# x's groups 8 to 11 ahead of Wv's second half, and a new order of the staged pieces

## The chip, the cores and the metric

One Trainium2 chip, 8 cores, one launch. Every core computes one of the 8 batch entries with the full weights, and no core talks to another. The metric is the device time in microseconds (us) of the slowest core. One core has TensorE (PE), VectorE (DVE), ScalarE (ACT), GpSimd (POOL) and SyncE (SP), and 16 DMA engines, which serve a queue of hardware-made transfers (issued here by SP) and one of software-made transfers (issued by GpSimd; these can cast f32 to bf16 on the way).

## What is computed

x is [8, 2048, 1024] f32. An adaptive-layernorm block: the vector c gives six modulation vectors, x goes through a linear attention with relu features, then through a quantized linear layer. Cut to what matters:

```python
mod = (silu(c) @ wmod).reshape(8, 6, 1, 1024)
sa, ca, ga, sb, cb, gb = (mod[:, k] for k in range(6))
ga, gb = (sign(g) * maximum(abs(g), 0.25) for g in (ga, gb))
h = layernorm(x) * (1 + ca) + sa
q = relu(h @ Wq.T) / 8;  k = relu(h @ Wk.T) / 8      # 16 heads of 64
v = h @ Wv.T;            u = silu(h @ Wu.T)
kv = k.T @ v             # per head, over all 2048 tokens
x = x + ga * ((srms_norm(q @ kv) * u) @ Wo.T)
h = layernorm(x) * (1 + cb) + sb
x = x + gb * (int8_linear(h, weight) + bias)
```

## The kernel before

A core's 2048 tokens are 16 groups of 128 (g), and four chunks of 512 (i). The first half of the kernel makes kv, which needs all tokens. For each chunk: `stats(g)` (VectorE, then three small GpSimd operations) and `xhat(g)` (ScalarE) normalize a group of x, `transp` turns it on TensorE into h1, `kproj` and `vproj` are eight products each (a unit is eight 128x512 matmuls into one PSUM bank, evicted by ScalarE), and `kvprod` adds to kv. The order of issue is written out by hand, and every engine works through its own instructions strictly in that order. In a loop over `eight`, unit n is (half, j): the first four units use the first half of the weight, the last four the second. The second half of the kernel makes Q, U, the heads, Wo, the second layernorm and the quantized layer chunk by chunk (`xunit`, `wproj`, `norm1`, `fproj`). Its first stage needs VectorE early: `qproj(0, ec)` is evicted by VectorE from ec = 2 on (L665), and the head product `ohead(0, 2)` (L692) needs that.

Three streams of loads lie around the change.

GpSimd issues, in this order: Wk's second half (four pieces), Wv's first half, x's groups 8 and 9, Wv's second half, groups 10, 11, 12 (L566 to L573); then, behind the statistics of groups 8 to 11, groups 13 to 15 as their buffers come free (`more_x`). A weight half is 2 MiB of f32 in HBM and is cast to bf16.

SP issues the staged pieces: 24 loads of 1 MiB in three buffers, in the order of the list `stream`: ga, sb, cb (four each), Wo (four), gb (four), the FFN weight (four). `AT` holds where each begins. The first three wait for Wv's first half (L575); each later one waits until the piece three before it is consumed (`staged`).

VectorE consumes them. `mod_piece(v, c)` multiplies a piece of wmod by silu(c) and sums it into a column (two operations, L436); after the fourth piece `mod_fin` finishes the vector. `wo_piece(c)` multiplies two rows of Wo's piece by ga (L479) and needs ga as a row, `row_g`. `ffn_quant` takes the last four. `mod()` takes the next entry of the list `mods` (16 wmod pieces with the four of Wo behind the twelfth). Before, it is called in all eight units of V of chunk 0, in all eight of V of chunk 1, and in the first four of K of chunk 2.

A finished column becomes a row of all partitions by `row(v, dst)`: a small DMA to HBM (`put`) and a broadcast back (`get`), both issued by GpSimd, with the wait for the put's landing between them. Before, `row(0)` stands in V of chunk 1, and between V of chunk 1 and K of chunk 2 stand Wq's first half, `row(1)`, Wq's second half, `row(2)` and both halves of Wu, all on GpSimd. `row(3)` goes into row_g again and therefore waits for the last Wo piece (`fold_tok`). `fill()` writes row_gbb to the whole output, four loads of SP behind the last FFN piece.

Of the kernel before, what the change touches and what calls it, by code (L numbers as in the profile page):

```python
# [13 lines left out]
D = 1024  # L14
# [3 lines left out]
NC = 8  # L18
# [54 lines left out]
def build_nc():  # L73
# [3 lines left out]
    def dram(name, shape, dt=F32, kind="ExternalInput"):  # L77
        return nc.dram_tensor(name, shape, dt, kind=kind)
# [8 lines left out]
    d_wb = dram("wmod_b", [128, 4, NC, D])  # L87
# [10 lines left out]
    def sb(name, shape, dt=F32, at=None):  # L98
        nbytes = int(np.prod(shape[1:])) * size[dt]
        off = cur[0] if at is None else at  # L100
        if at is None:
            cur[0] = off + ((nbytes + 31) // 32) * 32
        assert off + nbytes <= CAP, f"SBUF overflow: {name} {off + nbytes - CAP}"
        return nc.alloc_sbuf_tensor_at(name, list(shape), dt, offset=off)
# [7 lines left out]
    wv = sb("wv_s", [128, 2, NC, 512], BF16)  # L112
    wq_at = cur[0]
    wq = sb("wq_s", [128, 2, NC, 512], BF16)
    wu = sb("wu_s", [128, 2, NC, 512], BF16)
    wo = sb("wo_s", [128, NC, D], BF16)
# [3 lines left out]
    row_g = sb("row_g", [128, D])  # L120
    row_cb = sb("row_cb", [128, D])
    row_sb = sb("row_sb", [128, D])
    row_gbb = sb("row_gbb", [128, D])
# [18 lines left out]
    mod_c = [sb(f"mod_c{v}", [128, NC]) for v in range(4)]  # L142
# [5 lines left out]
    gbb_c = sb("gbb_c", [128, NC])  # L148
# [66 lines left out]
    def x_prev(g):  # L215

        return g - 2 * XR if g - XR in xe else g - XR

    def load_x(q, key, g, after):
        s = key % XR  # L220
        if key in xe:
            x_tok[key] = q.dma(sl_e[key], xe[key][:], bass.AP(d_x, g * 128 * D, [[D, 128], [1, D]]), *after)
            return
        x_tok[key] = q.dma(sl_x[q][s], xr[s][:],
                           bass.AP(d_x, g * 128 * D, [[D, 128], [1, D]]), *after)

    w_tok = {}
# [7 lines left out]
    def load_w(w, dst, hf, *after):  # L235
        w_tok[w, hf] = POOL.dma(sl_w[w, hf], dst[:, hf],
                                bass.AP(d_w[w], hf * NC * 512,
                                        [[2 * NC * 512, 128], [512, NC], [1, 512]]), *after)
# [1 line left out]
    st_tok = {}  # L240
    st_free = {}
    wa_free = {}
    stream = ([(d_wb, (v * NC + 2 * c) * D, 4 * NC * D) for v in range(3) for c in range(4)]
              + [(d_wo, 2 * c * D, NC * D) for c in range(4)]
              + [(d_wb, (3 * NC + 2 * c) * D, 4 * NC * D) for c in range(4)]
              + [(d_fw, 2 * c * D, NC * D) for c in range(4)])
    AT = {"ga": 0, "sb": 4, "cb": 8, "wo": 12, "gb": 16, "ffn": 20}

    def load_stage(n, *after):

        if n < len(stream):
            src, off, row = stream[n]
            st_tok[n] = SP.dma(sl_s[n % SR], stage[n % SR][:], bass.AP(src, off, [[row, 128], [1, 2048]]),
                               st_free.get(n - SR), wa_free[NC - 1], *after)

    def staged(n, t):

        st_free[n] = t
        load_stage(n + SR)
# [52 lines left out]
    def xhat(g):  # L312

        i, j = divmod(g, 4)
        x = xbuf(g)
        xh_tok[g] = x_free[g] = ACT.do(lambda e: e.activation(  # L316
            out=xh[j][:], in_=x[:], func=AF.Identity, scale=rt[j][:, 0:1], bias=nmr[j][:, 0:1]),
            nm_tok[g], tp_tok.get((i - 1, 3)), t_silr if g < 2 else None)
# [42 lines left out]
    def take():  # L361
        b = ring["banks"][ring["n"] % len(ring["banks"])]
        ring["n"] += 1
        return b, ring["free"].get(b)

    def mm8(lhs, rhs, bank, *after, each=None):
        for dc in range(NC):
            t = PE.do(lambda e, dc=dc: e.matmul(pb[bank][:], lhs(dc), rhs(dc),  # L368
                                                start=(dc == 0), stop=(dc == NC - 1)),
                      *after, each(dc) if each else None, inc=(dc == NC - 1))  # L370
        return t
# [5 lines left out]
    def kbuf(i, j):  # L377
        return kT1[j] if i == 1 else kT[j]
# [29 lines left out]
    def vproj(i, hf, j):  # L408
        b, free = take()
        t = vp_tok[i] = mm8(lambda dc: h1[:, i, dc, 128 * j:128 * j + 128], lambda dc: wv[:, hf, dc],  # L410
                            b, free, w_tok["wv", hf])
        v_tok[i, j] = ring["free"][b] = ACT.do(lambda e: e.copy(  # L412
            out=vT[j][:, 512 * hf:512 * hf + 512], in_=pb[b][:]), t, kv_tok.get((i - 1, j)))

    def kvprod(i, j):
        for p in range(NC):
            t = PE.do(lambda e, p=p: e.matmul(
                pb[p // 4][:, 128 * (p % 4):128 * (p % 4) + 128],
                kbuf(i, j)[:, 128 * p:128 * p + 128], vT[j][:, 128 * p:128 * p + 128],
                start=(i == 0 and j == 0 and p % 4 == 0),  # L420
                stop=(i == NT - 1 and j == 3 and p % 4 == 3)),
                k_tok[i, j], v_tok[i, j], k_free[0], k_free[1], inc=(p == NC - 1))
        kv_tok[i, j] = t
# [3 lines left out]
    row_tok, col_tok = {}, {}  # L427
    fold_tok = [None]
    put_tok = {}

    def mod_piece(v, c):

        n = AT[("ga", "sb", "cb", "gb")[v]] + c
        s = stage[n % SR]
# [7 lines left out]
    def put(k, col, *after):  # L442

        put_tok[k] = POOL.dma(sl_p[k], bass.AP(d_rows, k * D, [[NC, 128], [1, NC]]), col[:], *after)

    def get(k, row, *after):

        row_tok[k] = POOL.dma(sl_g[k], row[:], bass.AP(d_rows, k * D, [[0, 128], [1, D]]),
                              put_tok[k], *after)
# [20 lines left out]
    def row(v, dst, *after):  # L470
        put(v, mod_c[v], col_tok[v])
        get(v, dst, *after)

    def wo_piece(c):

        n = AT["wo"] + c
        s = stage[n % SR]
        for d in range(2):
            t = DVE.do(lambda e, d=d: e.tensor_tensor(  # L479
                out=wo[:, 2 * c + d], in0=s[:, 1024 * d:1024 * d + 1024], in1=row_g[:], op=ALU.mult),  # L480
                st_tok[n], row_tok[0])
        fold_tok[0] = t
        staged(n, t)
# [3 lines left out]
    def ffn_quant(ec):  # L487

        c, d = divmod(ec, 2)
        n = AT["ffn"] + c  # L490
        w = stage[n % SR][:, 1024 * d:1024 * d + 1024]
# [70 lines left out]
    def more_x(g):  # L562
        load_x(POOL, g, g, (x_free[x_prev(g)],))
# [2 lines left out]
    for c in range(4):  # L566
        load_wk(1, c, wa_tok[6, 1])
    load_w("wv", wv, 0)
    for g in (8, 9):
        more_x(g)  # L570
    load_w("wv", wv, 1)
    for g in (10, 11, 12):
        more_x(g)  # L573
    for n in range(SR):
        load_stage(n, w_tok["wv", 0])  # L575

    def piece(v, c):
        mod_piece(v, c)
        if c == 3:
            mod_fin(v)  # L580

    mods = [lambda v=v, c=c: piece(v, c) for v in range(4) for c in range(4)]
    mods[12:12] = [lambda c=c: wo_piece(c) for c in range(4)]

    def mod():
        if mods:
            mods.pop(0)()
# [5 lines left out]
    for n, (hf, j) in enumerate(eight):  # L593
        vproj(0, hf, j)
        if 1 < n < 6:
            xhat(6 + n)
            if n < 5:
                more_x(11 + n)
        mod()
        if n >= 5:  # L600
            kvprod(0, n - 5)
    for n, (hf, j) in enumerate(eight):
        vproj(1, hf, j)
        if n == 0:
            kvprod(0, 3)
        if n >= 5:
            kvprod(1, n - 5)
        if n < 4:
            transp(2, n)
            stats(12 + n)  # L610
        if n == 3:
            row(0, row_g)
        mod()

    load_w("wq", wq, 0, wa_free[NC - 1])
    row(1, row_sb)
    load_w("wq", wq, 1)
    row(2, row_cb)
    for h in range(2):
        load_w("wu", wu, h)  # L620
    for n, (hf, j) in enumerate(eight):
        kproj(2, hf, j)
        if n == 0:
            kvprod(1, 3)
        if n < 4:
            mod()
        else:
            xhat(8 + n)
    row(3, row_g, fold_tok[0])
    put(4, gbb_c, col_tok[3])  # L630
    get(4, row_gbb)
    for n, (hf, j) in enumerate(eight):
        vproj(2, hf, j)
        if n >= 5:
            kvprod(2, n - 5)
        if 1 < n < 6:
            transp(3, n - 2)
# [396 lines left out]
```

How the kernel before makes its waits and increments, by code:

```python
    def emit(self, eng):  # L47
        seen = {}
        for after, fn, sem, step in self.items:
            need = {}
            for s, v in after:
                if v > need.get(s.name, (s, 0))[1]:
                    need[s.name] = (s, v)
            for s, v in need.values():
                if v > seen.get(s.name, 0):
                    eng.wait_ge(s, v)
                    seen[s.name] = v
            if fn is None:
                continue
            ins = fn(eng)
            if sem is not None:
                ins.then_inc(sem, step)
```

## Time and profile before

| | |
|---|---|
| time, median of 3 runs | 458.42 us (458.16 to 458.9) |
| the profiled execution | 458.85 us; its slowest core's span 457.3 us |
| spans of the 8 cores | 450.7 to 457.3 us |
| TensorE busy | 390.0 us, 85% of the span |
| VectorE, ScalarE, GpSimd busy | 60%, 52%, 21% |
| HBM read, written | 70.36 MB, 24.67 MB |
| chain that ended last | PE 45%, DMA 17%, VectorE 13%, ScalarE 7% |

The profile is that of one execution; times in it are microseconds from the core's first instruction, and are those of the slowest core (core 4) where no other is named. The DMA share is the mean busy share of the core's 16 DMA engines. A number in brackets behind an instruction is the idle time of its engine just before it, and what ended that.

### The profile page before, as it was taken

What the parts mean: (1) busy time and instruction counts of PE and PEld (TensorE: products, weight loads), DVE (VectorE), ACT (ScalarE), POOL (GpSimd) and SP (SyncE); (2) the same over time, 40 slices, a digit from 0 to 9 for tenths busy, and PEclk for the clock granted to TensorE, in tenths of its full rate; (3) what the DMA queues carried; (4) which work ended last, traced back from release to release, by engine and by line L of the source; (5) the groups of instructions that cost most, each with busy time, mean ns of one, the idle gap of its engine ahead of it and who ended that gap; (6) DMA issues with size and microseconds to landing.
All of it is one profiled execution on the core that took longest, in us unless ns stands there. A gap on an engine that the chain in (4) does not pass through costs nothing.

```text
span 457.3 us, 6430 instructions; the slowest of 8 cores (450.7 to 457.3 us)
## 1 busy us (share of the span) xinstructions
PE 390.0 (85%) x2022; PEld 185.4 (41%) x2062; DVE 273.9 (60%) x487; ACT 235.6 (52%) x342; POOL 96.9 (21%) x148
## 2 busy tenths in 40 slices
PE   3043799849998999988898899999999999999983
PEld 1020444425544545434443344444444443444432
DVE  4557902175692644467845875568565755766885
ACT  3342553527257433768656854476825577443532
POOL 2514701040064011000011202121212131202421
PEclk9995699979999999998999999999999999999999
DMA  7999699949985999999698615634564574265796
GB/s 194 280 262 335 159 171 245 330 131 299 339 303 185 195 311 292 216 245 352 200 365 273 130 46 96 137 84 101 93 120 93 110 139 85 64 128 94 125 149 140
DMA packets 20914, 87.05 MB, mean 190 GB/s; under 512 B 2825, under 2 KB 3089, under 8 KB 17042
## 3 DMA queue, kind: packets, MB, share of 16 engines
q0 software_dynamic: 8544, 31.49, 37.9%
q1 hardware_dynamic: 12338, 55.16, 36.0%
q8 instruction: 17, 0.28, 0.3%
q14 instruction: 15, 0.12, 0.1%
HBM read 70.36 MB, written 24.67 MB: 208 GB/s over the span
## 4 chain that ended last, share of the span: by engine, by line
PE 45%; DMA 17%; DVE 13%; issue 8%; ACT 7%; SPq 6%; POOL 3%; DVEq 0%; ACTq 0%; POOLq 0%
PE pb L368 32%; PE pb L842 8%; DMA xr<-x_tm 8%; SPq L44 6%; DMA wa<-wmod_a 5%; DMA stage<-wmod_b 5%; DVE stage L436 3%; ACT rn L704 2%; DVE h L790 2%; DVE am L793 2%; DVE wm_c L492 2%; PE pb L702 1%; DVE bn L302 1%; ACT rn L707 1%; PE pb L819 1%
## 5 line engine op out<-in xcount | busy, mean ns | idle before, releaser
L368 PE MATMUL pb<-h,wu_s 128*128 128x512 bf16 x251 | 61.5, 386 | 1.6 <-ACT u_s L681 1.2
L368 PE MATMUL pb<-wo_s,u_s 128*128 128x512 bf16 x251 | 59.4, 379 | 1.2 <-DVE u_s L684 1.0
L842 PE MATMUL pb<-fq,xqT 128*128 128x512 bf16 (+1 forms) x255 | 58.7, 372 | 1.7 <-ACT xqT L824 1.3
L368 PE MATMUL pb<-wv_s,h 128*128 128x512 bf16 x249 | 59.2, 387 | 0.9 <-ACT kT L384 0.4
L368 PE MATMUL pb<-h,wq_s 128*128 128x512 bf16 x249 | 59.6, 379 | 0.4
L436 DVE SCALAR_TENSOR_TENSOR stage<-stage,silr 128x1024 f32<-128x1024 f32 x32 | 37.7, 1219 | 20.8 <-DMA stage<-wmod_b 20.8
L368 PE MATMUL pb<-wk_s,h 128*128 128x512 bf16 x203 | 45.4, 379 | 0.6 <-DMA wk_s<-wk 0.3
L709 DVE SCALAR_TENSOR_TENSOR q_s<-rn,pb 128x512 bf16<-128x512 f32 x32 | 22.0, 686 | 29.7 <-ACT rn L707 29.3
L302 DVE BATCH_NORM_STATS2 bn<-xr 128x6 f32<-128x512 f32 x26 | 16.7, 684 | 37.0 <-DMA xr<-x_tm 37.0
L368 PEld LDWEIGHTS pb<-h,wu_s 128*128 128x128 bf16 x256 | 24.9, 99 | 31.1 <-issue 4.5
L368 PEld LDWEIGHTS pb<-wo_s,u_s 128*128 128x128 bf16 x256 | 24.9, 98 | 31.0 <-issue 1.4
L368 PEld LDWEIGHTS pb<-h,wq_s 128*128 128x128 bf16 x256 | 24.8, 98 | 28.9 <-issue 0.2
L842 PEld LDWEIGHTS pb<-fq,xqT 128*128 128x128 bf16 x264 | 25.1, 98 | 27.6 <-issue 1.7
L368 PEld LDWEIGHTS pb<-wv_s,h 128*128 128x128 bf16 x256 | 24.7, 99 | 28.2 <-issue 2.7
L681 ACT ACTIVATE u_s<-pb 128x512 bf16<-128x512 f32 x32 | 18.6, 593 | 26.3 <-PE pb L368 26.2
L669 ACT ACTIVATE q_s<-pb 128x512 bf16<-128x512 f32 x26 | 15.5, 596 | 31.4 <-PE pb L368 23.6
L316 ACT ACTIVATE xh<-xr,nmr,rt 128x1024 bf16<-128x1024 f32 x13 | 16.1, 1240 | 29.9 <-POOL nmr L308 29.9
L412 ACT CAST vT<-pb 128x512 bf16<-128x512 f32 x32 | 18.4, 585 | 25.1 <-PE pb L368 25.0
L368 PEld LDWEIGHTS pb<-wk_s,h 128*128 128x128 bf16 x208 | 20.1, 98 | 24.1 <-issue 0.8
L44 POOL DMA_DIRECT2D out_tm<-h x15 | 13.5, 897 | 76.7 <-DVE h L846 63.0
L384 ACT ACTIVATE kT<-pb 128x512 bf16<-128x512 f32 x26 | 15.5, 596 | 27.3 <-PE pb L368 27.3
L305 POOL TENSOR_SCALAR rt<-mv 128x1 f32<-128x1 f32 x16 | 9.9, 618 | 88.6 <-DVE mv L304 87.0
(104 smaller groups left out, 577.2 us busy)
## 6 DMA issues: line engine op xcount, KB each, us to landing
stage<-wmod_b SPq DMA_DIRECT2D x16, 1024.0 KB, 11.6
xr<-x_tm SPq DMA_DIRECT2D x21, 512.0 KB, 4.6
wa<-wmod_a SPq DMA_DIRECT2D x16, 512.0 KB, 20.7
out_tm<-row_gbb SPq DMA_DIRECT2D x4, 2048.0 KB, 17.4
out_tm<-xr POOLq DMA_DIRECT2D x15, 512.0 KB, 7.9
out_tm<-h POOLq DMA_DIRECT2D x15, 512.0 KB, 5.3
xr<-x_tm POOLq DMA_DIRECT2D x8, 512.0 KB, 19.8
stage<-wo SPq DMA_DIRECT2D x4, 1024.0 KB, 6.2
```

The lines of the kernel that those rows point to most:

```text
L44: lambda e: e.dma_start(out=out, in_=in_, **how), slot.sem, 16))
L302: t = DVE.do(lambda e, hf=hf: e.bn_stats(out=bn6[j][:, 6 * hf:6 * hf + 6], in_=x[:, 512 * hf:512 * hf + 512]), x_tok[g])
L305: t = POOL.do(lambda e: e.tensor_scalar(out=rt[j][:], in0=mv[j][:, 1:2], scalar1=1e-5, scalar2=None, op0=ALU.add), t, xh_tok.get(g - 4))
L316: xh_tok[g] = x_free[g] = ACT.do(lambda e: e.activation(out=xh[j][:], in_=x[:], func=AF.Identity, scale=rt[j][:, 0:1], bias=nmr[j][:, 0:1] ...
L368: t = PE.do(lambda e, dc=dc: e.matmul(pb[bank][:], lhs(dc), rhs(dc), start=(dc == 0), stop=(dc == NC - 1)), *after, each(dc) if each else ...
L384: k_tok[i, j] = ring["free"][b] = ACT.do(lambda e: e.activation(out=kbuf(i, j)[:, 512 * hf:512 * hf + 512], in_=pb[b][:], func=AF.Relu, sc ...
L412: v_tok[i, j] = ring["free"][b] = ACT.do(lambda e: e.copy(out=vT[j][:, 512 * hf:512 * hf + 512], in_=pb[b][:]), t, kv_tok.get((i - 1, j)))
L436: col_tok[v] = DVE.do(lambda e, d=d: e.scalar_tensor_tensor(out=s[:, D * d:D * d + D], in0=s[:, D * d:D * d + D], scalar=1.0, in1=silr[:], ...
L669: q_tok[i, ec] = ring["free"][b] = ACT.do(lambda e: e.activation(out=q_s[:, ec], in_=pb[b][:], func=AF.Relu, scale=0.125), t, vp_tok[NT - ...
L681: u_tok[i, ec] = ring["free"][b] = ACT.do(lambda e: e.activation(out=u_s[i % 2][:, ec], in_=pb[b][:], func=AF.Silu), t, vp_tok[NT - 1], kv ...
L709: ot_tok[n] = o_free[b] = DVE.do(lambda e: e.scalar_tensor_tensor(out=q_s[:, p], in0=rn[n % 2][:], scalar=1e12, in1=pb[b][:], op0=ALU.min, ...
L842: t = PE.do(lambda e, ic=ic, sl=sl, ps=ps: e.matmul(ps, xqT[a][:, ic], fq[:, ic, sl], start=(ic == 0), stop=(ic == NC - 1)), free, xqT_tok ...
```

## The change

x's groups 10 and 11 are issued before Wv's second half, and the staged pieces wait for Wv's second half instead of its first. In the stream, gb's pieces stand ahead of Wo's. `mod()` is called in the last three units of V of chunk 0, the last four of V of chunk 1 (behind the statistics of groups 12 to 15), in all eight units of K of chunk 2 and in V of chunk 2 until the list is empty. The rows and the loads of Wq and Wu are issued within these loops: row 0 and Wq's first half in the fifth unit of V of chunk 1, row 1 and Wq's second half in the first unit of K of chunk 2, row 2 and both halves of Wu in its fifth, the puts of gb and of gb x bias with the get of row_gbb in the first unit of V of chunk 2, and the get of gb's row in its fifth. Nothing is added to the computation and nothing taken from it.

```diff
--- before.py
+++ after.py
@@ -240,11 +240,10 @@
     st_tok = {}
     st_free = {}
     wa_free = {}
-    stream = ([(d_wb, (v * NC + 2 * c) * D, 4 * NC * D) for v in range(3) for c in range(4)]
+    stream = ([(d_wb, (v * NC + 2 * c) * D, 4 * NC * D) for v in range(4) for c in range(4)]
               + [(d_wo, 2 * c * D, NC * D) for c in range(4)]
-              + [(d_wb, (3 * NC + 2 * c) * D, 4 * NC * D) for c in range(4)]
               + [(d_fw, 2 * c * D, NC * D) for c in range(4)])
-    AT = {"ga": 0, "sb": 4, "cb": 8, "wo": 12, "gb": 16, "ffn": 20}
+    AT = {"ga": 0, "sb": 4, "cb": 8, "gb": 12, "wo": 16, "ffn": 20}
 
     def load_stage(n, *after):
 
@@ -566,13 +565,12 @@
     for c in range(4):
         load_wk(1, c, wa_tok[6, 1])
     load_w("wv", wv, 0)
-    for g in (8, 9):
+    for g in range(8, 12):
         more_x(g)
     load_w("wv", wv, 1)
-    for g in (10, 11, 12):
-        more_x(g)
+    more_x(12)
     for n in range(SR):
-        load_stage(n, w_tok["wv", 0])
+        load_stage(n, w_tok["wv", 1])
 
     def piece(v, c):
         mod_piece(v, c)
@@ -580,7 +578,7 @@
             mod_fin(v)
 
     mods = [lambda v=v, c=c: piece(v, c) for v in range(4) for c in range(4)]
-    mods[12:12] = [lambda c=c: wo_piece(c) for c in range(4)]
+    mods += [lambda c=c: wo_piece(c) for c in range(4)]
 
     def mod():
         if mods:
@@ -596,8 +594,8 @@
             xhat(6 + n)
             if n < 5:
                 more_x(11 + n)
-        mod()
         if n >= 5:
+            mod()
             kvprod(0, n - 5)
     for n, (hf, j) in enumerate(eight):
         vproj(1, hf, j)
@@ -608,29 +606,35 @@
         if n < 4:
             transp(2, n)
             stats(12 + n)
-        if n == 3:
+        else:
+            mod()
+
+        if n == 4:
             row(0, row_g)
-        mod()
-
-    load_w("wq", wq, 0, wa_free[NC - 1])
-    row(1, row_sb)
-    load_w("wq", wq, 1)
-    row(2, row_cb)
-    for h in range(2):
-        load_w("wu", wu, h)
+            load_w("wq", wq, 0, wa_free[NC - 1])
     for n, (hf, j) in enumerate(eight):
         kproj(2, hf, j)
         if n == 0:
             kvprod(1, 3)
-        if n < 4:
-            mod()
-        else:
+        if n > 3:
             xhat(8 + n)
-    row(3, row_g, fold_tok[0])
-    put(4, gbb_c, col_tok[3])
-    get(4, row_gbb)
+        mod()
+        if n == 0:
+            row(1, row_sb)
+            load_w("wq", wq, 1)
+        if n == 4:
+            row(2, row_cb)
+            for h in range(2):
+                load_w("wu", wu, h)
     for n, (hf, j) in enumerate(eight):
         vproj(2, hf, j)
+        mod()
+        if n == 0:
+            put(3, mod_c[3], col_tok[3])
+            put(4, gbb_c, col_tok[3])
+            get(4, row_gbb)
+        if n == 4:
+            get(3, row_g, fold_tok[0])
         if n >= 5:
             kvprod(2, n - 5)
         if 1 < n < 6:
```

## Rows read from the trace of the kernel before

**Rows 1.** Spans of the cores, and mean granted TensorE clock.

```profile
core 2: 455.2 us, clock 0.966
...
core 4: 457.3 us, clock 0.966
```

**Rows 2.** Timeline, TensorE, core 4: start, us, operation, [idle before <-releaser].

```profile
77.53 10.52 PE L368 MATMUL pb<-wv_s,h 128*128 128x512 bf16 x47
...
92.22 0.61 PE L417 MATMUL pb<-vT,kT 128*128 128x128 bf16 x8 [1.99 <-ACT vT L412]
...
100.16 1.01 PE L417 MATMUL pb<-vT,kT 128*128 128x128 bf16 x8 [5.61 <-ACT vT L412]
...
100.97 3.62 PE L368 MATMUL pb<-wv_s,h 128*128 128x512 bf16 x8
...
141.90 0.44 PE L326 MATMUL pb<-id_b,xh 128*128 128x128 bf16 x5 [1.31 <-ACT xh L316]
```

**Rows 3.** Timeline, ScalarE, core 4.

```profile
98.30 1.24 ACT L316 ACTIVATE xh<-xr,nmr,rt 128x1024 bf16<-128x1024 f32 x1 [6.23 <-POOL nmr L308]
```

**Rows 4.** Timeline, VectorE, core 4, group 11's statistics.

```profile
91.94 1.29 DVE L302 BATCH_NORM_STATS2 bn<-xr 128x6 f32<-128x512 f32 x2 [3.27 <-DMA xr<-x_tm]
```

**Rows 5.** Timeline, GpSimd, core 4: loads issued, one small result.

```profile
53.73 0.56 POOL L44 DMA_DIRECT2D wv_s<-wv  x1
...
55.29 0.60 POOL L44 DMA_DIRECT2D wv_s<-wv  x1
...
55.81 1.65 POOL L44 DMA_DIRECT2D xr<-x_tm  x3
...
96.47 1.74 POOL L308 TENSOR_SCALAR nmr<-mv,rt 128x1 f32<-128x1 f32 x1 [0.18 <-POOL rt L307]
...
98.15 1.69 POOL L44 DMA_DIRECT2D xr<-x_tm  x3
```

**Rows 6.** Landings of the two loads of Wv (tile wv_s), core 4.

```profile
DMA to landing us min/median/max: 16.8/21.6/26.4
```

**Rows 7.** Windows: three of core 4, two of core 2; clock, DMA share, GB/s last.

```profile
60.00:90.00 30.00, 29.53 (x141) 13.48 (x142) 4.49 (x9) 12.77 (x21) 2.92 (x8) 1.00 1.01 254
...
90.00:105.00 15.00, 7.40 (x41) 3.79 (x40) 10.45 (x18) 4.24 (x6) 5.96 (x7) 0.77 0.52 165
...
122.00:155.00 33.00, 30.98 (x189) 15.89 (x191) 19.37 (x36) 19.16 (x28) 12.81 (x16) 1.00 0.82 244
...
90.00:105.00 15.00, 8.38 (x50) 4.55 (x49) 11.41 (x23) 3.41 (x5) 5.68 (x6) 0.77 0.64 185
...
122.00:155.00 33.00, 31.88 (x193) 16.45 (x196) 19.40 (x34) 19.15 (x28) 12.79 (x16) 1.00 0.82 221
```

**Rows 8.** Timeline, VectorE: last staged piece, first Q eviction; core 4, then 2.

```profile
183.56 1.22 DVE L436 SCALAR_TENSOR_TENSOR stage<-stage,silr 128x1024 f32<-128x1024 f32 x1
...
189.75 0.69 DVE L665 TENSOR_SCALAR q_s<-pb 128x512 bf16<-128x512 f32 x1 [3.58 <-PE pb L368]
...
182.28 1.22 DVE L436 SCALAR_TENSOR_TENSOR stage<-stage,silr 128x1024 f32<-128x1024 f32 x1
...
187.22 0.69 DVE L665 TENSOR_SCALAR q_s<-pb 128x512 bf16<-128x512 f32 x1 [2.33 <-PE pb L368]
```

**Rows 9.** DMA queues in 122:140, 147:156 and 189:208: packets, MB, share.

```profile
q1 hardware_dynamic: 797, 5.79, 89.8%
...
q0 software_dynamic: 237, 1.29, 87.1%
...
q0 software_dynamic: 285, 1.81, 54.0%
...
q1 hardware_dynamic: 549, 3.01, 46.6%
```

**Rows 10.** Timeline, GpSimd, core 4: the get of row_cb.

```profile
180.44 0.54 POOL L44 DMA_DIRECT2D row_cb<-rows  x1 [18.71 <-DMA rows<-mod_c]
```

**Rows 11.** Timeline, TensorE, core 4: third head product.

```profile
192.30 0.38 PE L692 MATMUL pb<-q_s,kv_bd 128*128 128x512 bf16 x1
```

## The prediction

> **What bounds the kernel now.** I began with the spans of the cores [rows 1]: core 4 is the slowest, core 2 stands 2.1 us below it. The profiled execution took 458.85 us, 1.55 more than core 4's span and 0.43 more than the median of the runs (458.42). The sums below are in core 4's span and are shifted at the end.
>
> Then TensorE in order of time [rows 2]. It is nearly full except around the first V product. There it stands still twice for an eviction of V, 1.99 and 5.61 us, and its granted clock is at the lower of its two levels afterwards, 1.2 GHz instead of 2.4: eight 512-column products take 3.62 us at 100.97, where 47 take 10.52 before (1.79 for eight), and eight small ones 1.01 instead of 0.61. A third wait, 1.31 us at 141.90, is for a normalized group.
>
> Who made the evictions late is seen one engine at a time. ScalarE [rows 3] stood 6.23 us in front of the normalization of group 11, and the V evictions queue behind it. That waited for GpSimd's small result, which ended at 98.2; it waited for VectorE's statistics, which waited for x's group 11 to land at 91.94 [rows 4]. Group 11 was issued at 55.8 with four others behind both halves of Wv [rows 5], and shared the last stretch with three staged pieces, released when Wv's first half landed (53.73 + 16.8 = 70.5) [rows 5, 6]. GpSimd could not issue groups 13 to 15 before 98.15, since they stand behind the late statistics.
>
> Last the windows [rows 7] and VectorE's order [rows 8]. The transfer engines are 0.52 busy in 90 to 105 and 0.82 in 122 to 155, and full in 60 to 90. In the second, VectorE waits for the row of ga with all three staged buffers full. So 15 x 0.48 + 33 x 0.18 = 7.2 + 5.9 = 13.1 us of transfer time are unused on core 4, 5.4 + 5.9 = 11.3 on core 2. The staged pieces end at 183.56 + 1.22 = 184.8 on VectorE, and the next thing in its order, the eviction of the third Q product, waits only 3.58 us for TensorE [rows 8]. This is the margin that matters: the staged pieces are a second path, just behind TensorE's.
>
> **The change part by part.** *Groups 10 and 11 ahead of Wv's second half.* Groups 8 and 9 follow Wv's first half (70.5) at once, groups 10 and 11 now follow them: four groups of half a MiB. A staged MiB costs 0.898 x 18 us = 16.2 us for 5.79 MB, 2.9 us [rows 9]; with the other stretches I take 3.1. So group 11 lands near 70.5 + 6.2 = 77, 15 us earlier, and ScalarE comes to it after six units, near 77.53 + 6 x 1.79 = 88. Both stalls (7.6 us) and the slow clock behind them (1.8 + 0.4 = 2.2) go. The price is that Wv's second half comes 3.1 us of transfer later. It landed at 55.3 + 26.4 = 81.7 + issue, about 82.2 [rows 5, 6], with three pieces taking part of the engines. Without them I put it at 81 to 82; it is wanted after four units, 77.53 + 4 x 1.79 = 84.7 [rows 2]. Margin 3 us; bounds are nothing and the 3.1 us minus that margin, so nothing.
>
> *Pieces only after Wv's second half.* The first leaves at 81 to 82 instead of 70.5. In a full queue this delays nothing by itself: what moves out of the way of one moves into the way of the other.
>
> *Pieces consumed from V's sixth unit, none before group 2's four statistics are done.* The pieces before those statistics are 3 instead of 12. In transfers, three pieces and groups 12 to 15 are 5 MiB, 82 + 5 x 3.1 = 97.5, so the statistics run near 98 to 105, ahead of ScalarE, which comes to them in the second half of K of chunk 2, near 117. The 1.31 us wait goes. VectorE's own work is the same; it is on no path here.
>
> *gb's pieces ahead of Wo's, row_g and the weights issued from within the loops.* ga is complete after the first piece behind the statistics, near 108, and row_g is back some 8 us later (an estimate, less than half of the 18.71 below, as no weight is ahead of it), long before Wo's pieces are due. The 5.9 us hole goes. On GpSimd each row is a put, a wait for its landing, a get and then the next weight load. The wait before row_cb was 18.71 us, with half a weight ahead of the put in the queue [rows 10]. By that, now: row_g and Wq's first half leave near 116; sb is complete near 117, its put lands behind Wq near 133; cb's near 152; then both halves of Wu leave, near 153 where it was 181. They are wanted near 192. puts 3 and 4 and their gets queue behind Wu, and nothing on GpSimd waits for them until the second layernorm. The output fill can start earlier, behind the last FFN piece in SP's order; it writes 8 MiB under products that wait for no load, so I cost it at nothing; if that cover is gone, the FFN piece is late, a MiB at 3.1 us.
>
> **The sum.** TensorE's path gains 7.6 + 2.2 + 1.3 = 11.1 us. Without more, the third Q product's eviction would be possible at 189.75 - 11.1 = 178.7, and the head product that needs it would come at 192.30 - 11.1 = 181.2 [rows 8, 11].
>
> VectorE's pieces end, by differences: 184.8 - 13.1 (holes) + 2 (new holes: the start behind Wv, the catch-up after the statistics) + what now goes ahead of the last Wo piece and did not before (both halves of Wu and row_cb) - 4 (FFN's first piece and the start of its second, which went ahead and no longer do). For Wu the row of 189 to 208 gives 0.54 x 19 = 10.3 us for 1.81 MB written, 5.9 us a half; that of 147 to 156 gives 0.871 x 9 = 7.8 us, less 1.6 for row_g, for 0.77 MB, 8.5 us a half [rows 9]. I take 6.5, nearer to the first, where both queues were at work as they will be; both halves 13, with row_cb 14.6. End: 184.3. Does all of Wu really go first? From 153 on both queues are loaded, the last row showing 54% to 47%; Wu's 14.6 us last some 29 us, and the five pieces left (15 us) as long. They end together, near 182, plus 2.3 us of VectorE.
>
> From that end, two VectorE operations of 0.69 us must precede the head product: 185.7 against 181.2. So 4.5 us are given back: 6.6 net, a span of 450.7. Core 2: its pieces ended at 182.28 + 1.22 = 183.5, it has 1.8 us less of holes: 183.5 - 11.3 + 2 + 14.6 - 4 = 184.8, plus 1.4 = 186.2. Its head product stood 2.55 us behind its eviction as on core 4, at 187.22 + 2.55 = 189.8 [rows 8, 11]. So 455.2 + 186.2 - 189.8 = 451.6, and core 2 becomes the slowest. Plus 1.55 for what lies around the span, minus 0.43 to stand at the median: **452.7 us**, 5.7 less than before. A new TensorE standstill of 4 to 5 us can drop the clock again; row 100.97 prices that at 2.2 us, but Q's stage is paced by ScalarE at 2.5 us a unit, so I leave it to the range.
>
> The Trainium skill ("DMA: Bandwidth & Descriptors", Anatomy of one DMA) fits a software-queue transfer as 2.0 us plus bytes over 436e3. With the 2.1 MB that half a weight reads, its data part would be 4.8 us a half, Wu 9.6, and by that rule the time would be 449.3, a weaker form of the first rival. The rows here say 5.9 to 8.5, so the trace does not agree with it in this stage, and I give it no more than that rival's chance.
>
> **The rivals.** *The pieces keep up (20%).* If Wu leaves later than 160 or takes the smaller share, the pieces end by 180 and the full 11.1 us stay: 457.3 - 11.1 + 1.55 - 0.43 = 447.3. For it: GpSimd's round trips are long and each step later takes Wu out of the pieces' way. Against: cb would have to be some 8 us later than I place it.
>
> *Most is given back (15%).* Wu's halves at 8.5 us add 4.0, the slow clock 2.2; one of them gives 454.9 or 456.7. For it: the one row at 8.5, and the drop after 5.61 us of standing. Against: the later rows, and ScalarE's pace.
>
> *Slower (9%).* All eight cores now stream without pause from 60 to 184; if that lowers the rate of each, the pieces pay it. The place is that stretch, 103 us from 81 on. At 10% less the price is 10.3 us: 463. It decides from about 5.5%, where the 5.7 us are gone. Against: in 60 to 90 the engines were at full share already, at 1.01 [rows 7].
>
> *The change does not do what it says (6%).* Wv's second half arrives late enough (88 or more) that one wait replaces the other and the pieces start later too: 457.5 to 459.
>
> The forecast holds 50%, with its own range 450.5 to 454.9. The range of 8 in 10 reaches from the first rival to the second: 447.0 to 457.5. A measurement of this kernel can't tell less than 0.2% (0.9 us) from no change. Faster than that: 0.50 + 0.20 + 0.14 = 0.84; within: 0.06; slower: 0.10.
>
> **What would show it.** In the changed profile: V's first product without a wait above 1 us and the clock full in 90 to 105; group 11's statistics before 82; the DMA share near 1 from 60 to 185; Wo's last piece on VectorE ending near 184; Wu issued near 153; TensorE waiting for VectorE's Q eviction in the Q stage for 3 to 5 us; core 2 nearly as long as core 4. The prediction is wrong if Wo's last piece ends before 180 (then 447), or if TensorE waits for Wv near 84.

## The result, and the profile after

The changed kernel takes 464.98 us in the median of four runs, where the kernel before takes 458.66 us beside it: the ratio is 1.0126, with a 95% interval of 1.0095 to 1.0158, so it is 1.3% slower. The forecast was 452.7 us, with a range of 447.0 to 457.5. It is wrong, in its sign too. (One of the four runs stood at 509 us, with one die at a granted clock near 0.82; it counts in the median and not in the ratio.)

The profiled execution took 464.71 us. First the cores; core 2 is the slowest in it, as forecast (in the three other runs it was core 1), and all rows below are of core 2 where no other is named.

```profile
core 2: 463.2 us, clock 0.956
...
core 4: 461.2 us, clock 0.958
```

TensorE's timeline, which answers to [rows 2], and with its last lines to [rows 11]:

```profile
77.08 10.53 PE L367 MATMUL pb<-wv_s,h 128*128 128x512 bf16 x48
...
87.88 1.89 PE L367 MATMUL pb<-wv_s,h 128*128 128x512 bf16 x8
...
101.37 3.62 PE L367 MATMUL pb<-wv_s,h 128*128 128x512 bf16 x16
...
179.12 0.38 PE L706 MATMUL pb<-osq,blk 128*128 128x512 bf16 x1 [0.19 <-ACT osq L698]
196.29 0.59 PE L696 MATMUL pb<-q_s,kv_bd 128*128 128x512 bf16 x1 [16.79 <-DVE q_s L713]
196.67 3.62 PE L367 MATMUL pb<-h,wq_s 128*128 128x512 bf16 x8
```

The first V product has no wait left and keeps its clock: 48 products in 10.53 us, then eight in 1.89, without a bracket, and sixteen of the second V product in 3.62 at 101.37. The next large wait is new: 16.79 us in front of the third head product. Behind it eight products take 3.62 us, as long as those sixteen: the granted clock is 0.50, which is 1.2 GHz. The head product waits for VectorE, whose timeline answers to [rows 8]:

```profile
171.35 2.36 DVE L478 TENSOR_TENSOR wo_s<-stage,row_g 128x1024 bf16<-128x1024 f32 x2 [3.22 <-DMA stage<-wo]
180.98 2.36 DVE L478 TENSOR_TENSOR wo_s<-stage,row_g 128x1024 bf16<-128x1024 f32 x2 [7.27 <-DMA stage<-wo]
189.94 2.36 DVE L478 TENSOR_TENSOR wo_s<-stage,row_g 128x1024 bf16<-128x1024 f32 x2 [6.60 <-DMA stage<-wo]
192.59 2.36 DVE L478 TENSOR_TENSOR wo_s<-stage,row_g 128x1024 bf16<-128x1024 f32 x2 [0.29 <-DMA stage<-wo]
194.86 0.69 DVE L669 TENSOR_SCALAR q_s<-pb 128x512 bf16<-128x512 f32 x1
```

The four pieces of Wo each wait for their transfer. The last ends at 192.59 + 2.36 = 194.95, and the Q eviction follows with no wait of its own. So the staged pieces are no longer just behind TensorE, they set the pace. In the windows (columns as in [rows 7]) the transfer engines are full from 120 on, while TensorE does nothing in 180 to 190:

```profile
80.00:90.00 10.00, 10.00 (x59) 4.95 (x57) 1.08 (x1) 7.61 (x10) 1.69 (x3) 1.00 0.71 220
...
100.00:110.00 10.00, 10.00 (x72) 5.51 (x70) 9.31 (x19) 5.21 (x9) 4.99 (x11) 1.00 0.87 319
110.00:120.00 10.00, 10.00 (x54) 4.76 (x53) 7.67 (x18) 3.44 (x7) 2.50 (x5) 1.00 0.77 231
120.00:140.00 20.00, 20.00 (x130) 10.56 (x129) 7.14 (x12) 15.44 (x22) 0.90 (x2) 1.00 0.99 239
...
180.00:190.00 10.00, 0.00 (x0) 0.00 (x0) 2.42 (x3) 0.91 (x2) 0.00 (x0) 0.67 0.98 254
190.00:200.00 10.00, 3.71 (x9) 1.41 (x10) 7.05 (x8) 0.60 (x1) 1.08 (x2) 0.50 1.02 295
```

GpSimd's timeline tells when Wu's two halves entered the queue, and the tile wu_s when they landed: 159.9 + 19.7 = 179.6 and 160.4 + 29.2 = 189.6.

```profile
111.75 0.65 POOL L44 DMA_DIRECT2D rows<-mod_c  x1 [0.78 <-DVE mod_c L462]
115.90 0.53 POOL L44 DMA_DIRECT2D row_g<-rows  x1 [3.51 <-DMA rows<-mod_c]
...
139.65 0.53 POOL L44 DMA_DIRECT2D row_sb<-rows  x1 [15.66 <-DMA rows<-mod_c]
...
159.36 0.53 POOL L44 DMA_DIRECT2D row_cb<-rows  x1 [11.16 <-DMA rows<-mod_c]
159.88 1.08 POOL L44 DMA_DIRECT2D wu_s<-wu  x2
```
```profile
DMA to landing us min/median/max: 19.7/24.5/29.2
```

Last, the balance of the transfer engines on core 2 from 72 us to the landing of the last piece ahead of the Q evictions, first before (72 to 181.1), then after (72 to 192.5); the columns are packets, MB and the share of the 16 engines' time.

```profile
q1 hardware_dynamic: 2947, 21.52, 60.3%
q0 software_dynamic: 1633, 6.97, 28.0%
```
```profile
q1 hardware_dynamic: 2973, 21.73, 56.3%
q0 software_dynamic: 2066, 9.56, 38.2%
```

Before, that is 65.8 us of SP's queue, 30.5 us of GpSimd's and 12.2 us of nothing in 109.1 us (the rest, 0.5%, is instruction fetches). After, 67.8, 46.0 and 6.1 us in 120.5. The change filled 6.1 us of holes and put 15.5 us of GpSimd's transfers (Wu and the row of cb), and 2.0 of SP's, ahead of the last piece. The sum 15.5 + 2.0 - 6.1 = 11.4 us is the difference of the two stretches and must come out so; it says how the delay is made up, and the pieces do end 194.95 - 183.50 = 11.45 us later. The delay is not that of one core: the mean end of the pieces over the eight cores moved from 179.7 to 190.0. That Wu is the cause was still to be tested.

### The profile page after: what moved, and what is told of

It is laid out like the page before. It is cut to its first block, busy times and chain, and to the rows that moved or that the text cites. A ratio compares the mean times of both kernels' runs of the same rounds, so it can differ in the third digit from the quotient of the medians.

```text
span 463.2 us, 6473 instructions; the slowest of 8 cores (452.8 to 463.2 us)
## 1 busy us (share of the span) xinstructions
PE 391.1 (84%) x2062; PEld 185.2 (40%) x2062; DVE 274.3 (59%) x487; ACT 236.0 (51%) x342; POOL 89.3 (19%) x148
## 4 chain that ended last, share of the span: by engine, by line
PE 35%; DMA 28%; DVE 13%; issue 7%; ACT 6%; SPq 6%; POOL 2%; DVEq 0%; ACTq 0%; POOLq 0%
PE pb L367 23%; DMA stage<-wmod_b 12%; PE pb L846 8%; DMA stage<-wo 7%; SPq L44 6%; DMA wv_s<-wv 6%; DMA wa<-wmod_a 5%; DVE stage L435 3%; ACT rn L708 2%; DVE wm_c L491 1%; DVE h L794 1%; DVE am L797 1%; PE pb L706 1%; DVE bn L301 1%; PE pb L823 1%
## 5 line engine op out<-in xcount | busy, mean ns | idle before, releaser
L367 PE MATMUL pb<-h,wq_s 128*128 128x512 bf16 x256 | 62.1, 387 | 0.0
L846 PE MATMUL pb<-fq,xqT 128*128 128x512 bf16 (+1 forms) x264 | 60.2, 373 | 1.1 <-ACT xqT L828 1.1
L673 ACT ACTIVATE q_s<-pb 128x512 bf16<-128x512 f32 x26 | 15.5, 596 | 31.4 <-PE pb L367 23.6
L383 ACT ACTIVATE kT<-pb 128x512 bf16<-128x512 f32 x26 | 15.5, 597 | 28.4 <-PE pb L367 28.4
L696 PE MATMUL pb<-q_s,kv_bd 128*128 128x512 bf16 x32 | 12.3, 385 | 20.5 <-DVE q_s L713 20.4
L811 ACT ACTIVATE xq<-h,cst,rs 128x1024 f16<-128x1024 f32 (+1 forms) x17 | 20.0, 1182 | 15.4 <-DVE rs L802 15.4
```

Of the source, the lines that this page charges most:

```text
L383: k_tok[i, j] = ring["free"][b] = ACT.do(lambda e: e.activation(out=kbuf(i, j)[:, 512 * hf:512 * hf + 512], in_=pb[b][:], func=AF.Relu, sc ...
L673: q_tok[i, ec] = ring["free"][b] = ACT.do(lambda e: e.activation(out=q_s[:, ec], in_=pb[b][:], func=AF.Relu, scale=0.125), t, vp_tok[NT - ...
L696: o_tok[i, p] = PE.do(lambda e: e.matmul(pb[b][:], kv_bd[:, p], q_s[:, p], start=True, stop=True), q_tok[i, p], t_kv[0], o_free.get(b))
L811: xq_tok[g] = xq_tok[g, k] = ACT.do(lambda e, sl=sl: e.activation(out=xq[a][:, sl], in_=h2[g % 4][:, sl], func=AF.Identity, scale=rs[a][:, ...
L846: t = PE.do(lambda e, ic=ic, sl=sl, ps=ps: e.matmul(ps, xqT[a][:, ic], fq[:, ic, sl], start=(ic == 0), stop=(ic == NC - 1)), free, xqT_tok ...
```

## The experiments

Theory A: TensorE's gain is real, and is given back because both halves of Wu now go ahead of the last staged pieces, which the Q evictions stand behind on VectorE. Rival B: the pieces are late since they start 11 us later, behind Wv's second half. Rival C: it is GpSimd's long chain of puts and gets, or the order of gb and Wo, and not Wu's bytes.

**Wu last** (e1_wu_last). The changed kernel, but Wu is issued when the last Wo piece is consumed:

```diff
             row(2, row_cb)
-            for h in range(2):
-                load_w("wu", wu, h)
...
         if n == 4:
+            for h in range(2):
+                load_w("wu", wu, h, fold_tok[0])
             get(3, row_g, fold_tok[0])
```

> The changed kernel with one thing moved: both halves of Wu are issued behind Wo's last piece instead of behind row_cb. Theory A (Wu's loads, now ahead of the last Wo pieces, hold them back, and the Q evictions stand behind those pieces in VectorE's order): Wo's last piece ends on VectorE near 183 instead of 195 (12 us of transfer time out of its way), TensorE's wait in the Q stage falls from 16.8 us to about 4, and the time falls from 465 to 452 to 456, the rest being a new wait for Wu near unit 8. Rival B (the pieces are late because they start 11 us later, behind Wv's second half): the pieces still end near 190, the wait stays above 10 us, the time stays at 461 or more.

Measured: 455.52 us, ratio to the kernel before 0.9935 [0.9912, 0.9957]. On its slowest core (core 1, 452.5 us) VectorE's last Wo piece and TensorE's waits are these:

```profile
178.00 2.36 DVE L478 TENSOR_TENSOR wo_s<-stage,row_g 128x1024 bf16<-128x1024 f32 x2 [1.01 <-DMA stage<-wo]
```
```profile
181.69 0.38 PE L696 MATMUL pb<-q_s,kv_bd 128*128 128x512 bf16 x1 [3.13 <-DVE q_s L713]
181.91 3.57 PE L367 MATMUL pb<-h,wq_s 128*128 128x512 bf16 x8
...
196.26 3.23 PE L367 MATMUL pb<-h,wu_s 128*128 128x512 bf16 x8 [2.56 <-DMA wu_s<-wu]
```

The pieces end 14.6 us earlier than in the changed kernel's core 2 (12.4 in the mean of the eight cores, 177.6 for 190.0), about the time that Wu takes (below), and 9.5 us come back. Against that stand a wait for Wu itself, 2.56 us here and 1.2 to 4.5 on the eight cores, and a slow clock behind both waits here. A holds.

**The early start** (e2_start_wv0). The changed kernel, but with the pieces' loads behind Wv's first half, as before:

```diff
-        load_stage(n, w_tok["wv", 1])
+        load_stage(n, w_tok["wv", 0])
```

> The changed kernel, but the staged pieces start behind Wv's first half again, as before the change. Rival B: the pieces end about 10 us earlier, near 185, and the time falls to about 455. Theory A: the queues are full, so an earlier start only fills the hole of 3 us at 82 to 86; the pieces end 2 to 4 us earlier and the time falls by 2 to 4 us, to 461 to 463.

Measured: 464.53 us, ratio 1.0135 [1.0116, 1.0153]: no better than the change, and above what either theory expected. The pieces end no earlier: between 186.6 and 193.5 on the eight cores, 191.2 in the mean, for 190.0 in the changed kernel. The head product still waits 6.6 to 12.5 us, and Wv's second half is late now, by 1.9 to 5.2 us, here on core 3:

```profile
85.80 5.70 PE L367 MATMUL pb<-wv_s,h 128*128 128x512 bf16 x16 [5.13 <-DMA wv_s<-wv]
```

Only the first three pieces can come earlier: VectorE takes the fourth behind the statistics of groups 12 to 15 in either kernel. B falls.

**Both** (e4_both): the two edits above together.

> The changed kernel with both: Wu behind Wo's last piece, and the pieces started behind Wv's first half. Theory A: 1 to 4 us below the run with Wu moved alone, so 449 to 454. Theory B: as the run with the early start alone, within 2 us.

Measured: 456.21 us, ratio 0.9951 [0.9934, 0.9968], not faster than the first edit alone; A had expected a further gain of 1 to 4 us, which did not come. TensorE waits 2.6 to 5.1 us on every core for Wv's second half, which cost it nothing in the first kernel of this section.

**Half of Wu** (e9_half_wu): the first half where the change has it, the second behind the last Wo piece.

```diff
-            for h in range(2):
-                load_w("wu", wu, h)
+            load_w("wu", wu, 0)
...
+            load_w("wu", wu, 1, fold_tok[0])
             get(3, row_g, fold_tok[0])
```

> The changed kernel with one half of Wu behind the last Wo piece, the other where the change has it. Theory A: half the dose, half the effect: the last Wo piece ends 5 to 7 us earlier than in the changed kernel, the Q wait is 8 to 11 us, the time is 459 to 461, between 465 and 455.5. Rival C (what hurts is GpSimd's place in line for Wu, not its bytes): as the changed kernel, 464 to 466.

Measured: 459.42 us, ratio 1.0009 [0.9993, 1.0024]. The last Wo piece of its slowest core (core 6):

```profile
187.96 2.36 DVE L478 TENSOR_TENSOR wo_s<-stage,row_g 128x1024 bf16<-128x1024 f32 x2 [1.50 <-DMA stage<-wo]
```

So with none, one and both halves ahead the pieces end at 180.4, 190.3 and 195.0 on the slowest cores (177.6, 184.8 and 190.0 in the mean of the eight), and the kernel takes 455.5, 459.4 and 465.0 us. The times follow the bytes, in two steps of 3.9 and 5.6 us, while the chain of puts and gets up to the row of cb is the same in all three: that much of C falls.

**The order of gb and Wo** (e7_wo_first): Wo's pieces ahead of gb's again, and Wu behind gb's last piece instead of Wo's. The puts of gb and of gb x bias, which need gb's column, move with it from V's first unit to its fifth.

```diff
-    mods += [lambda c=c: wo_piece(c) for c in range(4)]
+    mods[12:12] = [lambda c=c: wo_piece(c) for c in range(4)]
...
+        if n == 4:
+            for h in range(2):
+                load_w("wu", wu, h, col_tok[3])
```

> The kernel with Wu behind the last staged piece (455.5), with the old order of the last eight pieces: Wo's ahead of gb's. Theory A: the number of bytes ahead of the last piece is the same, only its name differs, so the Q stage's wait stays at 2 to 5 us and the time within 1.5 us of 455.5. If the order itself (gb first) were what cost time, 452 or less.

Measured: 454.74 us, ratio 0.991 [0.9885, 0.9935], beside 455.52 and 0.9935 for the other order (intervals that overlap). The order is worth nothing that these runs can tell.

**Wu without company** (e8_wu_alone): as Wu last, and x's first loads for the second half of the kernel wait on SP until Wu has landed.

> The kernel with Wu behind the last piece, with the five loads of x for the second half held until Wu has landed (they left together and share the engines). Theory A (transfer engines full around 180 to 200): Wu lands some 3 us earlier, its wait of 1.6 to 2.6 us before the first U unit goes, the time is 452 to 454 instead of 455.5. If the two queues do not hurt each other there, no change.

Measured: 455.22 us, ratio 0.993 [0.9906, 0.9953]. TensorE's waits for Wu remain, at 1.4 to 3.0 us, and core 3 waits 4.84 us at 222, in the quantization of the FFN weight. The gain of 2 to 3 us that A expected did not come; these runs give no sign that x's loads were what held Wu up.

**x's order alone** (e3_x_only): the kernel before with the first part of the change and nothing else.

```diff
     load_w("wv", wv, 0)
-    for g in (8, 9):
+    for g in range(8, 12):
         more_x(g)
     load_w("wv", wv, 1)
-    for g in (10, 11, 12):
-        more_x(g)
+    more_x(12)
```

> The kernel before with the first part of the change alone: x's groups 8 to 11 ahead of Wv's second half; pieces, their order and the weights as before. Theory A: the two waits in V of chunk 0 (1.99 and 5.61 us) and the slow clock go, the pieces end near 178 since the transfer hole at 90 to 96 closes, and Wu stays behind them, so most of the gain arrives: 448 to 451. Theory B has no other number here. If instead the statistics of groups 12 to 15, still behind 8 to 11 pieces, hold up group 2's normalization, TensorE waits 3 to 8 us at the start of V of chunk 2 and the time is 452 to 456.

Measured: 453.91 us, ratio 0.9907 [0.9884, 0.9931], already 11 us under the changed kernel. The time lies in the second of the ranges expected, but not for its reason: nothing waits at V of chunk 2. The price is a wait for Wv's second half, from 1.92 us on core 0 to this on core 3, with part of what follows at 1.2 GHz:

```profile
90.19 4.98 PE L368 MATMUL pb<-wv_s,h 128*128 128x512 bf16 x16 [5.61 <-DMA wv_s<-wv]
```

**Two parts** (e6_parts_1_2): the same with the pieces' start behind Wv's second half.

> The kernel before with the first two parts: x's groups 8 to 11 ahead of Wv's second half, and the pieces started behind that half. The order of the pieces, their places on VectorE, the rows and the weights as before. Theory A: the wait for Wv's second half that the first part alone brought (4 to 5.6 us) goes; but VectorE now reaches the statistics of groups 12 to 15 only behind pieces that start 11 us later, so TensorE waits 5 to 12 us for group 3's normalization at V of chunk 2, and the time is 454 to 460, no better than the first part alone (453.9). If that wait does not come, 449 to 451.

Measured: 455.53 us, ratio 0.9935 [0.9913, 0.9957]. The waits of the first V product are gone, and the late start costs elsewhere. VectorE comes to the statistics of groups 12 to 15 behind the eight pieces of the first V product, ScalarE's normalization is late, and evictions behind it too. TensorE on the slowest core (core 5):

```profile
124.32 1.89 PE L368 MATMUL pb<-wv_s,h 128*128 128x512 bf16 x8 [0.72 <-ACT kT L384]
...
128.24 1.89 PE L368 MATMUL pb<-wv_s,h 128*128 128x512 bf16 x8 [2.03 <-ACT kT L384]
```

Two more follow, 1.96 and 1.31 us. So the start behind Wv needs fewer pieces ahead of those statistics, as the change has.

**Fewer pieces ahead of the statistics** (e10_stats_early): the last kernel, with three `mod()` moved from the first V product to the third K product.

```diff
-        mod()
+        if n >= 3:
+            mod()
         if n >= 5:
             kvprod(0, n - 5)
...
-        if n < 4:
-            mod()
-        else:
+        if n > 3:
             xhat(8 + n)
+        if n < 7:
+            mod()
```

> Before, with the first two parts of the change (x's groups 8 to 11 ahead of Wv's second half, staged pieces behind that half), the old order of the pieces and the old places of Wu's load, and one thing more: the first three places of the first V product hold no piece, and the three pieces so displaced stand in the fourth to seventh unit of the third K product, so that the statistics of x's groups 12 to 15 stand behind three pieces fewer on VectorE. In the kernel with the two parts alone TensorE lost about 6 us at 124 to 136 us to the scaling of those groups (0.72, 2.03, 1.96 and 1.31 us on the slowest core), and its transfers were otherwise ahead. Theory A (the change loses only by Wu's halves in front of the last pieces and by what stands in VectorE's order; TensorE's gain is real): those waits go, and the kernel takes 448 to 452 us, ratio 0.978 to 0.986 to the kernel before. Rival (the transfers' total sets the end, so that any wait removed early comes back late): 454 to 456 us, with a wait of the third x block's Q product, or of the head or U product, that is longer by what was gained.

Measured: 449.86 us (447.75 to 450.52), ratio 0.9808 [0.9784, 0.9833]: 1.9% faster than the kernel before and, by the two ratios (0.9808 / 1.0126), 3.1% than the changed one. Wu leaves at 172.4, and gb's last load left at 159.7. VectorE's last piece and the Q eviction behind it, then the head product, on its slowest core (core 0, 448.6 us):

```profile
175.85 1.22 DVE L436 SCALAR_TENSOR_TENSOR stage<-stage,silr 128x1024 f32<-128x1024 f32 x1
...
178.39 0.69 DVE L665 TENSOR_SCALAR q_s<-pb 128x512 bf16<-128x512 f32 x1
```
```profile
179.82 0.38 PE L692 MATMUL pb<-q_s,kv_bd 128*128 128x512 bf16 x1 [0.30 <-DVE q_s L709]
```

The head product is at 179.82 and waited 0.30 us. So the pieces keep up with TensorE here, and to within 1.9 us on all eight cores, and TensorE's gain is kept. TensorE's wait for Wu is 0.7 us on this core and 2.3 on core 3.

This kernel is also 5.7 us faster than Wu last, though Wu leaves 8.5 us earlier in it on the slowest cores (172.4 for 180.9). What can be read: its pieces end at 174.9 in the mean of the eight cores, for 177.6 there, the longest wait of the head product is 1.9 us for 3.5, and three cores wait for Wu, 0.7 to 2.3 us, where there all eight do. The two kernels differ in the order of the stream, in the places of the pieces and in those of the rows, and no run separates these.

**The same with the early start** (e11_stats_early_wv0), the pieces behind Wv's first half:

> The same kernel with the staged pieces' loads behind Wv's first half, as in the kernel before, instead of the second. Theory A: a wait of 3 to 5 us for Wv's second half comes back on TensorE in the first V product, and pieces end earlier by 1 to 2 us, which are worth nothing as long as the Q product doesn't wait: 452 to 455 us, 2 to 4 us over the variant with the later start. Rival (the transfers' total sets the end): no difference between the two, or this one is faster, since its pieces start 5 us earlier.

Measured: 454.34 us, ratio 0.9904 [0.9885, 0.9924], 4.5 us over the last. Core 1, its slowest, waits 4.8 us for Wv's second half. With the statistics out of the way, the start behind Wv's second half is worth 1%; without that (the two kernels before) it cost more than it gave, by 1.6 us, with intervals of the two ratios that overlap.

## Why the prediction was wrong

**What held.** *TensorE's gain*, forecast as 11.1 us. Group 11's statistics, wanted before 82, ended by 77.1; the waits of V and the slow clock are gone. On core 4 the head product could have come at 179.1 (193.38, less its wait of 14.26), where 181.2 was forecast; on core 2 at 179.5, 10.3 us ahead of the 189.8 of before. Over the eight cores this gain is between 5.7 and 14.4 us, 10.1 in the mean. The best kernel above shows that it can be kept. *Wv's second half* landed at 56.0 + 25.7 = 81.7, forecast 81 to 82, and nothing waited. *Wu's cost*: the shares of the queues from 159.9 to 189.6, while Wu was under way, are

```profile
q0 software_dynamic: 492, 2.63, 51.5%
q1 hardware_dynamic: 630, 4.61, 48.6%
```

That is 15.3 us for Wu and row_cb in GpSimd's queue, forecast 14.6. By the fit in the Trainium skill ("DMA: Bandwidth & Descriptors", Anatomy of one DMA) the data part of Wu would be 9.6 us, an estimate. With 1.6 off for row_cb the trace has 13.7, so here too it does not agree. *That all of Wu goes ahead*: its second half landed at 189.6, ahead of the last piece, and GpSimd's queue had 51.5% to SP's 48.6%, where 54% to 47% was taken. The Trainium skill ("DMA: Bandwidth & Descriptors", Queues, rings and completion order) says that an engine takes turns between its queues, a packet from each. The nearly even shares of time agree with turns; the packets that the profile counts, 492 to 630, don't show them. *That TensorE stands in the Q stage for VectorE's eviction.* That core 2 was the slowest of the profiled run is in part luck: in the three other runs core 1 was, and the cores change places from one execution to the next.

**What failed** is one step, the end of VectorE's pieces: 184.8 forecast for core 2, 194.95 measured. Held against the balance above, by its own terms (forecast, then measured, us): SP's transfers that went ahead before and no longer do, -4 and +2.0; Wu and the row, +14.6 and +15.5; holes, -11.3 + 2 = -9.3 and -6.1. The errors are 6.0, 0.9 and 3.2, together 10.1. So the path and the wait were right, and what failed is the size of two terms of the sum, what FFN's pieces give back and the holes.

The largest is the "-4" for FFN. The twenty pieces ahead of the Q evictions are 20.97 MB; so of the 21.52 MB before only 0.55 were FFN's, 1.7 us at 3.06 us per MB, not 4. And after, FFN's first piece leaves at 183.8, when the second Wo piece is consumed, and 0.76 MB (2.4 us) are again ahead of the last Wo piece: three buffers in turn always let the next stream in two pieces early, whichever order the stream has. So nothing goes away. The rest of the 2.0, 1.3 us, is a price per MB that rose from 3.06 to 3.12 us.

The holes left were 6.1 us instead of 2 (and those of before 12.2, where the two windows of the prediction showed 11.3). In the windows above they are 0.29 x 10 = 2.9 us at the start of the pieces (80 to 90), and 1.3 and 2.3 in 100 to 120. There VectorE had the statistics of groups 12 to 15, which ended at 107.8, ahead of the buffers that it had to empty.

What follows is the prediction's own chain. Its head product on core 2 was at 186.2, a wait of 6.7 us against the 179.5; with 10.1 more that is 16.8, the wait in the trace. The span should then be 451.6 + 10.1 = 461.7; it is 463.2, and the slow clock accounts for about the 1.5 left: the next head product comes 4.17 us behind the one that waited (200.46), where it came 2.51 us behind it before. I had priced it at 2.2 and left it to the range.

**The rivals.** The one on the other side, 9%, gave 463 for a transfer rate 10% lower. It has nearly the time, but not the mechanism: SP's price per MB rose by 2%, 1.3 us of the 10.1. "The pieces keep up" had as its condition that Wu leaves after 160, and then an end by 180; Wu left at 159.9, and the pieces ended 15 us after 180, so the condition was set wrong. GpSimd's steps from sb's put on were 6 to 7 us behind the forecast (139.65 for 133, 159.36 for 152, 159.9 for 153), but the pieces were late as well, so that Wu still met all four of Wo's. I had given 0.84 to faster because the margin of the pieces was taken as a difference of estimates near 185 on both paths, while each of its five terms could be off by 3 us; an error of 10 us in such a sum was not in the range.

**The whole, in one line.** The change frees about 10 us on TensorE and moves 15.5 us of transfers, of which Wu's 13.7 are not wanted before 192, ahead of transfers that are wanted at 178.

## What to carry to other kernels

Filling holes in the transfers helps only the transfers wanted next. Before a load is moved earlier, list by their due times what it is moved ahead of; here, with the engines full, 15.5 us of moved transfers and 11.4 us of delay of the load behind them went together (6.1 us of holes were filled, 2.0 us of SP's came on top). To cost a second path, sum over its whole stretch by queue (bytes, share, holes) and check the sum on the kernel before; a difference of single terms from short rows hid 6 us here. And take the parts of a change apart: the first two, with the statistics early enough, gave 1.9%, and the change as a whole is a loss of 1.3%. Of the 15.1 us between these two kernels Wu's early load is 9.5; the other 5.7 are not taken apart.

## What the runs showed of the hardware

- While Wu's two loads and the row of cb shared the engines with SP's pieces (changed kernel, core 2, 159.9 to 189.6), GpSimd's queue had 51.5% of the engines' time and SP's 48.6%, although only the former's loads cast on the way. From 160 to 180 it was 54.0% to 46.9%.
- A MB of SP's pieces cost 2.79 us of the engines' time with nothing of GpSimd's beside it (before, core 4, 122 to 140: 89.8% of 18 us for 5.79 MB), and 3.13 us beside Wu (48.6% of 29.7 us for 4.61 MB).
- A put of 4 KB by GpSimd landed within 4 us of its issue when the loads before it had long been issued (put at 111.75, get at 115.90), and took 21.3 us behind both halves of Wu in the same queue (issued at 169.2).
- A clock of 1.2 GHz, for all or most of the next eight products, came after waits of 2.19 us (Wu last, core 6, 181.89) and 3.13 us (core 1, 181.69). It did not come after the waits of 0.72 and 2.03 us in the kernel with two parts, nor after one of 3.16 us in the kernel with the early start (core 7, 86.54: sixteen products in 3.61 us). So the length of the wait alone does not decide it. After the wait of 16.79 us the products at 196.67 ran at 1.2 GHz and those at 200.68 (1.89 us for eight) at 2.4 again.
- The cores of the changed kernel, which do the same work, differ by 10.4 us in one execution (452.8 to 463.2), and in the wait for the head product they reach from 9.9 to 16.8 us. They differ by pairs: of cores 0 and 1, 2 and 3, 4 and 5, 6 and 7 one has its last piece done by 188.7, the other at 192.0 or later. Before, the even cores ended at 182.3 to 184.8 and the odd ones at 174.4 to 178.9. Which of a pair is ahead changes from run to run; no run here shows why.
